# A graph network's first layer: its row gathers wait for the gather three in front, not two

## The reference

```python
h = relu(layernorm(x))                         # (12500, 16)
e = relu(edge_attr @ W1 + b1)                  # 412500 x 256
w_edge = (e @ W2 + b2).reshape(-1, 16, 16)
msgs = einsum('ei,eio->eo', h[src], w_edge)    # a row of h for each edge
aggr = segment_sum(msgs, dst, num_segments=12500)
out = aggr + h @ root + bias                   # then batch norm, relu, residual
```

## Time and profile before

| | |
|---|---|
| time, median of 3 runs | 8332.26 us (8326.56 to 8350.35) |
| profiled execution | 8296.17 us, span 8294.4 us |
| granted TensorE clock over the span | 0.949 |
| PE busy | 7333.8 us (88%) |
| DVE busy | 6680.6 us (81%) |
| POOL busy | 5653.6 us (68%) |
| ACT busy | 4443.1 us (54%) |
| first layer's groups | from about 62 to 5042 us of the span |

### The profile page before, as it was taken

The page is one execution under the profiler, slowest core; times in us unless marked ns, Lnnn a source line. Parts: engine busy times, 40 slices in busy tenths (PEclk is TensorE's granted clock), DMA queues, the critical chain, the costliest instruction groups (busy, mean ns, idle before and its releaser), DMA issues. The chain is left out here.

```text
span 8294.4 us, 193483 instructions
## 1 busy us (share of the span) xinstructions
PE 7333.8 (88%) x52997; PEld 6345.0 (76%) x52997; DVE 6680.6 (81%) x17449; ACT 4443.1 (54%) x8279; POOL 5653.6 (68%) x4866
## 2 busy tenths in 40 slices
PE   6888887888888888888888886999999999999998
PEld 5666666666666666666666665999999999999996
DVE  6667776777677777777777767999999999999997
ACT  4333343333333333333333434888888877778884
POOL 5656665666566666665666664888888888888886
PEclk8999999999999999999999998999999999999999
DMA  2111111111111111111111114445555555555544
GB/s 59 17 17 17 17 17 16 17 17 17 17 17 17 17 17 17 17 17 17 17 17 17 17 17 100 75 73 75 75 73 75 73 73 73 72 73 74 75 73 65
DMA packets 713464, 341.73 MB, mean 41 GB/s; under 512 B 422115, under 2 KB 656599, under 8 KB 713427
## 3 DMA queue, kind: packets, MB, share of 16 engines
q0 software_dynamic: 332928, 64.86, 13.5%
q1 hardware_dynamic: 379313, 272.94, 13.3%
q10 hardware_dynamic: 1186, 3.51, 0.1%
HBM read 307.85 MB, written 32.96 MB: 41 GB/s over the span
## 5 line engine op out<-in xcount | busy, mean ns | idle before, releaser
L803 POOL DMA_INDIRECT xg<-gather_rows,idx x3132 | 3001.6, 958 | 1996.5 <-issue 1259.3
L920 PE MATMUL ps_w<-W2s,hT 128*128 128x256 f32 x12928 | 3244.2, 406 | 63.0 <-issue 33.9
L920 PEld LDWEIGHTS ps_w<-W2s,hT 128*128 128x128 f32 x12928 | 2632.5, 205 | 627.7 <-issue 126.7
L1746 POOL DMA_INDIRECT sums<-total,row x1616 | 2548.8, 1577 | 541.8 <-issue 487.7
L1709 PE MATMUL ps_wide<-hot_col,placed 128*128 128x392 f32 x12928 | 2436.4, 345 | 9.1 <-DVE placed L1545 3.2
L1709 PEld LDWEIGHTS ps_wide<-hot_col,placed 128*128 128x128 f32 x12928 | 2315.3, 196 | 19.1 <-issue 12.8
L842 ACT ACTIVATE hT<-ps_h,b1c 128x512 f32<-128x512 f32 x1616 | 1024.7, 680 | 2288.5 <-remote 1662.2
L1003 DVE TENSOR_TENSOR prod<-ps_w,xg 128x512 f32<-128x512 f32 x1616 | 1082.2, 689 | 326.2 <-issue 66.1
L906 PE MATMUL ps_h<-eT,W1p 96*128 96x512 bf16 x1616 | 526.8, 407 | 656.3 <-ACT eT L836 480.1
L1644 ACT ACTIVATE square<-iota_col,minus_col 128x784 bf16<-128x784 int16 x1212 | 1061.2, 938 | 74.1 <-issue 57.6
L1545 DVE SCALAR_TENSOR_TENSOR placed<-ps_r,src_r,halves 128x512 fp32r<-128x512 f32 x1616 | 1099.1, 746 | 0.1
(11 more groups left out here) (229 smaller groups left out, 5613.6 us busy)
## 6 DMA issues: line engine op xcount, KB each, us to landing
dst_row<-dst_rows SPq DMA_DIRECT2D x404, 256.0 KB
src_row<-src_rows SPq DMA_DIRECT2D x404, 128.0 KB
xg<-gather_rows,idx POOLq DMA_INDIRECT x3132, 2.4
q_win<-q_rows SPq DMA_DIRECT2D x404, 96.0 KB
ea<-in_edge_attr SPq DMA_DIRECT2D x404, 64.0 KB
sums<-total,row POOLq DMA_INDIRECT x1616
e<-in_edge_attr SPq DMA_DIRECT2D x404, 32.0 KB
q_rows<-Q SPq DMA_DIRECT2D x12, 768.0 KB, 5.1
```

The costliest lines, as they stand in the source:

```text
L803: pool.indirect_dma_start(xg[r][:, t, :], None, k.rows, bass.IndirectOffsetOnAxis(ap=idx[r][:, t:t + 1], axis=0)).then_inc(xg_in[r][t], 16)
L920: last = pe.matmul(to, hT[half][:, j, col:col + P], k.W2[:, j, :], start=(j == 0), stop=(j == 1 and not with_b2))
L1746: pool.indirect_dma_start(k.sums[t], bass.IndirectOffsetOnAxis(ap=row[r][:, t:t + 1], axis=0), total[r][:, t, :], None, compute_op=ALU.add ...
```

## The change

A gather waits for the gather three in front of it in the group, from the fourth gather on. Before, it waited for the one two in front, from the third on. The wait of the third gather and its count of `gathers_begun` are gone; the number of gathers, the ring, and the waits for indices and messages stay.

```diff
                     for t in range(T - 1 if dense(r, use) else T):
-                        if t >= 2:
-                            pool.wait_ge(xg_in[r][t - 2], 16 * (use + 1))
+                        if t >= 3:
+                            pool.wait_ge(xg_in[r][t - 3], 16 * (use + 1))
                             pool.sem_inc(q["gathers_begun"], 1)
                         pool.indirect_dma_start(
                             xg[r][:, t, :], None, k.rows,
```

## The result

The changed kernel takes 9190.67 us (9186.48 to 9196.56, 4 runs) against 8337.55 us (8326.56 to 8350.35, 4 runs) for the kernel before, run beside it. The ratio is 1.1023, with a 95% interval from 1.1004 to 1.1042: 10% slower. The prediction said 8329 us, with a range up to 8360 and 79 in 100 for no change. It was wrong. The profiled execution took 9186.48 us, span 9184.8.

A forecast was written before the change was run, and what follows sets the result against it. It took the loop of TensorE, ScalarE and VectorE to bound the first layer: zero gain after 300 us, 3 us before it, so 8332 became 8329 us, range 8292 to 8360.

The forecast's parts named there:

- GpSimd's part: First layer's gathers: a full group falls from 11.9 to 10.0 us, own waits (713.8 us) to near nothing.
- the lead: First layer after 300 us: GpSimd runs 19 gathers ahead, some 25 us, so the change is worth zero there.
- the loop that TensorE and ScalarE keep costs as much by itself: First 300 us: groups with gather waits take 12.18 us, later ones 13.09 and 12.26, so little is gained.
- rival 4: Denser gathers slow VectorE at the shared SBUF interfaces: 0.19 us a group, 77 us in all, 8409 us; 7%.
- Rival 5: Three gathers in flight land later, so the deeper wait brings nothing: no change, 8332 us; 7%.
- Rival 3: GpSimd sets the first layer's pace after all: minus 713.8 us, 7618 us; 1%.
- The clock: Early groups: TensorE's clock rises where waits go, another 0.05 giving 14.6 us, 8312 us in all; 7%.

The follow-up runs named there:

- session 5: Runs sent together on one chip: changed kernel beside the kernel before, TensorE's semaphore counts on time; 7331.39 us against 8154.63, ratio 0.8991.
- session 1: The main comparison, changed kernel beside the kernel before on one chip, TensorE's semaphore counts late: 9190.67 us against 8337.55, ratio 1.1023.
- session 6: Kernel before profiled again, 8152.16 us, counts late; beside it, gathers replaced by plain DMAs with memsets (7375.1 us) or by memsets alone (7993.71 us).
- pairs of session 3: Changed kernel plus an 830-element GpSimd memset behind the second, fourth and sixth gather of a group: 8094.98 us against 8155.15 for the kernel before, 0.9923.
- even gaps: Changed kernel plus a 256-element GpSimd memset behind every gather: 9184.14 us, ratio 1.1105 to the kernel before.
- sessions 3: Kernel before (8155.15 us) beside four variants: gathers paced in pairs by memsets, or replaced by memsets or by plain DMAs from GpSimd or SyncE; counts on time.
- the single drain: Kernel before with its waits inside a group replaced by one, the fifth gather's for the fourth to land: 8266.64 us, ratio 0.9992.
- session 4: Changed kernel again, counts late, 9181.82 us against 8316.42, 1.1024; beside it, gathers in pairs with memsets of 830 (8413.73 us) or 450 elements (9133.9 us).

## Why the prediction was wrong

**GpSimd's part: right.** Gathers 1.25 us apart, the fourth hardly waiting, a burst of 9.0 us from first to last start, no waits of VectorE, the own waits down by 500 us. The waits for indices rose by 1760 us instead of 1000, because the groups became longer. The message of group 16 was to start within 10 us of 283.1 and starts at 327.1; in session 5 it starts at 248.2.

**The step that failed** is "After 300 us the value is therefore zero: what hides it is the lead". The lead was read rightly: nobody waited for a gather. But it shows only that the landing of a gather costs nothing. That its issue acts on nobody was assumed. In session 1 each group paid 2.26 us for it, 16% of the new group, with no row that names a gather as what was waited for. The prediction had one sentence for the case, "that would mean that GpSimd's pattern acts on the other engines without being waited for, which no row here prices well", and gave it no chance of its own.

**The step under it** is "the loop that TensorE and ScalarE keep costs as much by itself", from three stretches of 12 to 13 us a group. All three contained gathers. Without them the loop takes 9.72 us. The row that said so stood in the text: ScalarE's 673.8 us until "remote" in 2000 us. I explained it with the code, as the two engines waiting for each other. With counts on time in session 5 no wait of the relu ends in "remote". All its waits in 2000 us are then 346.7 us, 1.7 us a group, and have TensorE's name; before, those with TensorE's name (210.2 us) and "remote" made 884 us, 5.4 a group. Most of that was held counts.

**The rivals.** The sign is that of rival 4 (denser gathers slow another engine), its mechanism is not: 0.11 us a group by the one-hots, and its 80 us on top of 8329 are a tenth of the loss. Rival 5 (three in flight land later) is out: landing takes 2.4 us in the median with gathers 1.25 us apart (session 5), so that the third in front has landed. Rival 3, "GpSimd sets the pace after all", with 1 in 100 and 7618 us, is what the kernel before does in session 6, where VectorE waits 442.3 us for gathers; where its counts are on time the changed kernel gains 823 us (session 5), more than that rival's 714.

**The clock.** It fell from 0.93 to 0.87 in the groups. The Trainium skill, TensorE: Matmul & The Clock Gate, What's actually happening, ties a throttled clock to idleness, and here the rows agree: TensorE was busy 84% of the stretch before (3810 of 4549 us) and 79% after (4269 of 5408). A group has 10.3 us of busy TensorE before and 11.5 after, so that about half of the 2.26 us at most are matmuls made longer at the lower clock. That the lower clock follows from the waits and doesn't cause them is argued: in the groups of the kernels where TensorE waits little it is 1.00 (no gathers; plain DMAs; the changed kernel in session 5), while the pairs of session 3, with all counts on time but VectorE waiting for gathers, stand at 0.94.

**What stays open.** What makes a session hold the counts isn't known; neither the chip nor the kernel's code decides it. The kernel before was not profiled in sessions 3 and 5, so whether its counts were late there isn't known either. One mark goes with it: in the four sessions with late counts the trace lacks two thirds of the landing counts of the second layer's scatters as well (before: 9020 of 25856 recorded), and in the other two nearly none (25537 of 25856 in session 5). Kernels without gathers lack them too and have no late counts, so the missing records alone aren't the cause. Whether the recording has a part in the hold, together with the gathers, wasn't tried; of the rivals left this is the nearest, since all traces with the mark and indirect gathers have late counts and none without the mark does. TensorE's own idle time in front of the edge weights isn't needed for the loss: with even gaps a group takes 14.49 us at 70.9 us of it, after the change 14.52 at 709.3. What the changed kernel does in a session like the sixth, and what the single drain does where counts are on time, wasn't run. Whether the count is held or the matmul ends late, and where, can't be told from modelled ends. That the indirect DMAs make the loss in these sessions, and that another pacing of them takes it back, is shown; that it is the pause itself which does it is the best reading of these runs and not the only one.

## What to carry to other kernels

An engine whose work nobody waits for can still set the pace, so "hidden" is worth testing once by leaving that work out: one run without the gathers would have shown 9.7 against 12.3 us a group. Idle time that ends in "remote" or "issue" is unexplained time and need not be the loop's own. And a wait in a queue of indirect DMAs is also a pause: before it is removed or deepened, keep one (here a drain after four gathers cost nothing, 0.9992), and compare in more than one session, since the same two kernels stood at 1.10 in two of them and at 0.90 in a third.

## What the hardware showed that I had not expected

- TensorE's semaphore counts came late while indirect DMAs followed each other, and ScalarE's and VectorE's didn't: the count of eT's source by 5.4 us in the median with gathers 1.25 us apart (session 1), by 2.5 us with pairs 1.25 and 1.57 us apart (session 4). The same instructions had all counts within 0.5 us in session 5.
- A pause of 0.9 us after every second gather gave nearly all of it back (12.60 us a group), one of 0.6 us next to nothing (14.39).
- Plain 128-row DMAs from GpSimd cost 536 ns each instead of 951, landed after 2.0 us instead of 2.4, and held nothing at 0.94 us apart.
- Memsets on one partition, one after another, made VectorE's bf16 one-hots 755 ns long instead of 281.
